# VectorE makes the first two one-hots of a stage before it waits for the chunk's dst sums and adds them

## The reference

```python
inv_dx = 1.0 / maximum(edge_attr_2[:, 0], 1e-6)
slope  = edge_attr_2[:, 1] * inv_dx
diff   = (x[dst] - x[src]) * inv_dx[:, None]
d1     = segment_sum(diff, dst) - segment_sum(diff, src)
S      = segment_sum(slope, dst)                  # the same for all features
x1     = layernorm(x + (x - clip(dt, 0.01, 2.0) * (x * d1 + g * S)))
mean   = segment_sum(edge_attr_16, dst) / max(count(dst), 1)
out    = layernorm(x1 + mean)
```

## Time and profile before

| | |
|---|---|
| median of three runs | 4510.34 us (4507.86 to 4515.13) |
| the profiled execution | 4508.76 us, of which 4506.9 us is the span from first to last instruction |
| granted TensorE clock, mean | 0.996 |
| TensorE matmul busy | 98% of the span |
| VectorE busy | 85% |
| GpSimd busy | 76% |
| ScalarE busy | 32% |
| first stage's head, last chunk's head | 56.1 us and 4418.8 us |

### The profile page before, as it was taken

The page is one execution under the profiler, slowest core; times in us unless marked ns, Lnnn a source line. Parts: engine busy times, 40 slices in busy tenths (PEclk is TensorE's granted clock), DMA queues, the critical chain, the costliest instruction groups (busy, mean ns, idle before and its releaser), DMA issues. The chain is left out here.

```text
span 4506.9 us, 73977 instructions
## 1 busy us (share of the span) xinstructions
PE 4409.8 (98%) x31379; PEld 1230.9 (27%) x12630; DVE 3846.0 (85%) x8605; ACT 1458.2 (32%) x1018; POOL 3430.4 (76%) x3133
## 2 busy tenths in 40 slices
PE   4999999999999999999999999999999999999997
PEld 1222222222222222222222222222222222222222
DVE  6888888888888888888888888888888888888887
ACT  4333333333333333333333333333333333333321
POOL 7777777777777777777777777777777777777770
PEclk9999999999999999999999999999999999999998
DMA  3111111111111111111111111111111111111110
GB/s 92 37 35 41 36 35 37 35 42 36 35 37 35 42 35 37 35 35 42 35 37 35 40 37 36 36 35 42 35 37 35 35 42 35 37 35 38 39 25 8
DMA packets 210291, 167.80 MB, mean 37 GB/s; under 512 B 124650, under 2 KB 193774, under 8 KB 210024
## 3 DMA queue, kind: packets, MB, share of 16 engines
q1 hardware_dynamic: 109798, 139.79, 10.1%
q0 software_dynamic: 100000, 25.80, 6.4%
q10 hardware_dynamic: 476, 2.01, 0.1%
HBM read 164.55 MB, written 2.81 MB: 37 GB/s over the span
## 5 line engine op out<-in xcount | busy, mean ns | idle before, releaser
L427 POOL DMA_INDIRECT x_src<-in_x_dram,src_i x3125 | 3425.4, 1096 | 961.5 <-issue 910.2
L653 PE MATMUL ps_src<-hi_hot,spread_lo 128*128 128x392 bf16 x18750 | 4125.1, 329 | 0.0
L1000 DVE TENSOR_SCALAR hi_hot<-col_h,hi_f,scale 128x1568 bf16<-128x1568 f16 x3125 | 2137.0, 703 | 23.9 <-PE ps_src L653 22.8
L648 PE MATMUL ps_src<-hi_hot,spread_lo 128*128 128x392 bf16 x6250 | 2048.9, 328 | 16.7 <-DVE hi_hot L1000 9.0
L648 PEld LDWEIGHTS ps_src<-hi_hot,spread_lo 128*128 128x128 f16 x6250 | 615.8, 99 | 1026.9 <-issue 648.0
L601 PEld LDWEIGHTS ps_w<-dst_hots,parts 128*102 128x102 bf16 x3125 | 392.5, 126 | 978.8 <-issue 939.3
L979 DVE TENSOR_TENSOR spread_lo<-spread_lo,halves 128x640 f16<-128x640 f16 x1250 | 601.7, 489 | 64.9 <-PE ps_src L653 64.8
L590 PEld LDWEIGHTS ps_x<-xwin,nodes_mem 112*128 112x128 bf16 x3125 | 301.4, 98 | 1197.6 <-issue 1187.8
L590 PE MATMUL ps_x<-xwin,nodes_mem 112*128 112x48 bf16 x3125 | 580.0, 188 | 13.7 <-ACT nodes_mem L530 13.7
L601 PE MATMUL ps_w<-dst_hots,parts 128*102 128x112 bf16 x3125 | 499.6, 213 | 4.0 <-DVE parts L908 4.0
L528 ACT ACTIVATE nodes_mem<-rel_all,row_neg 128x3200 bf16<-128x3200 f16 x125 | 370.2, 2962 | 393.1 <-PE ps_x L590 390.6
(11 more groups left out here) (119 smaller groups left out, 1110.8 us busy)
## 6 DMA issues: line engine op xcount, KB each, us to landing
rel_all<-rel_d SPq DMA_DIRECT2D x125, 800.0 KB
x_src<-in_x_dram,src_i POOLq DMA_INDIRECT x3125
a<-in_edge_attr_dram SPq DMA_DIRECT2D x125, 200.0 KB, 2.4
a<-in_edge_attr_dram SPq DMA_DIRECT2D x125, 25.0 KB
src_i<-in_src_dram SPq DMA_DIRECT2D x125, 12.5 KB, 1.9
dst_i<-in_dst_dram SPq DMA_DIRECT2D x125, 12.5 KB, 1.7
xwin<-xparts_d SPq DMA_DIRECT2D x125, 10.5 KB
dst_sum<-in_dst_dram SPq DMA_DIRECT2D x1, 1400.0 KB
```

Source lines behind the costliest of these rows:

```text
L427: nc.gpsimd.indirect_dma_start(x_src[:, b, j * F:(j + 1) * F], None, x[:, :], bass.IndirectOffsetOnAxis(ap=src_i[:, b, j:j + 1], axis=0)). ...
L648: return nc.tensor.matmul(out_bank, weights, moving, start=False, stop=stop)
L653: return nc.tensor.add_instruction(mybir.InstMatmult(name=nc.get_next_instruction_name(), engine=pe.engine, start_tensor_calc=False, stop_ ...
L1000: v.tensor_scalar(hi_hot[:, slot(j), :], col_h[:, :], hi_f[:, b, j:j + 1], scale[:, b, j:j + 1], ALU.is_equal, ALU.mult).then_inc(hi_hot_r ...
```

## The change

The call of `add_window` moves from ahead of the loop over j to behind one-hot 1. The register loads stay where they are. Everything that follows one-hot 1 in the stage keeps its order. The last chunk's own code (below the loop) is untouched.

```diff
+        WINDOW_AT = 1
...
                 dve.wait_ge(dve_step, base_step)
                 if tiles:
                     load_stage(c + 1)
-                    add_window(c, b, base_step)
-                    done["window_rel"] = count[0]
                 for j in range(J):
                     if tiles:
                         one_hot(c, b, j)
+                        if j == WINDOW_AT:
+                            add_window(c, b, base_step)
+                            done["window_rel"] = count[0]
                         late(c, j)
```

## The result

The changed kernel takes 4537.39 us (median of 4 executions, 4527.70 to 4540.58) against 4512.74 us for the kernel before (now the median of four, with 4517.24 as the fourth): 1.0055 times as long, 95% interval 1.0042 to 1.0069. That is slower, clear of noise, and outside the forecast range of 4504 to 4518. The profiled execution has a span of 4535.8 us, 28.9 more than before. By the heads of the stages, 1.8 us of it come up before stage 2, 27.1 us in the 122 stages from 2 to 123 (35.296 instead of 35.074 us each), nothing behind them.

The account below looks back on a forecast made before the run. TensorE's own work was taken to bound the kernel at 35.07 us a stage. Zero for TensorE and zero for the path at start and end gave 4510 us, own range 4507 to 4514, wider range 4504 to 4518.

Parts of the forecast that it names:

- What bounds the kernel: Whole run: TensorE's own work sets the stage at 35.07 us; VectorE has about 4.8 us idle in each.
- Do the one-hots fit?: Stage's head: moved one-hots start near 2032.5, end some 1.0 us before the sums; add stays at 2034.90, cost nothing.
- What VectorE gains: From one-hot 2 on VectorE may run 1.2 us earlier, given back at one-hot 20; its end of stage doesn't move.
- the wait before one-hot 20: Late in VectorE's stage: one-hot 20, come 1.2 us earlier, would wait about 1.1 us for tile 12.
- The gathers: GpSimd's gathers beside the moved one-hots: zero on balance, bounds -0.1 and +0.73 us of GpSimd's time a stage.
- Cost: 0: At the diff: 1.2 us earlier it waits 0.75 us for gathers; up to 2.7 us late is free for TensorE.
- Rival 2: GpSimd becomes the bound: stretched gathers delay the diff in all stages, 0.48 us a stage, 59 us, 4569 us; chance 0.12.
- Rival 1: TensorE's small waits, 4.8 us outside the first fill, go: 4505 to 4510 us, middle 4507; chance 0.10.
- Rival 3: Diff waits 1 to 3 us in all stages instead of 37; 3 us more, up to 8: 4513 to 4518; chance 0.10.
- Middle stages that are not 35.07 us apart: Sign of a wrong prediction; the gathers' mean against 1.097 and the diff's place against 2.7 us then test rival 2.

Follow-up runs that it names:

- scratch reduction: The kernel before with one extra 1.2 us tensor_reduce, its result unread, between the register loads and the wait for the dst sums: 4506.96 us, 0.9986 of the kernel before.
- run 5: The kernel before with the two spreads behind one-hots 2 and 3 moved behind one-hot 8, so the diff comes 0.8 us earlier: 4548.68 us, 1.0068 of the kernel before.

## Why the prediction was wrong

**What bounds the kernel.** TensorE, with VectorE idle 4.8 us a stage: right for the kernel before. The same part noted GpSimd's 35.0 us beside TensorE's 35.07, but as a remark to the gathers and not as a second bound.

**Do the one-hots fit?** The start near 2032.5, when tile 17 is done, was wrong. One-hot 0 starts on average 1.8 us behind the last slope (122.4 + 32.8 us in 86 waits, by the third and fourth row of VectorE's waits above), and in each of these stages within 0.14 us of the last register instruction, so it is these that it waits for and not TensorE, which the third row names. The register loads of `load_stage`, which stayed ahead of the one-hots, take that time on VectorE and were hidden under the wait of 3.8 us. So there is no 1.0 us between one-hots and add; the add follows at once and is itself up to some tenths late. Nobody waits for it, so this cost nothing here, as argued.

**What VectorE gains.** In the stage shown it did run ahead by 1.5 us up to the diff, and the wait before one-hot 20 doesn't appear, as the diff ate the lead first.

**The gathers: the step that failed.** The prediction wrote: "I take zero on balance, with bounds of -0.1 and +0.73 us of GpSimd's time a stage." It is +0.24: 25 gathers of 1.106 instead of 1.097, 27.66 us instead of 27.42. With 25 x 0.305 us between them that is 35.3 against TensorE's 35.07, and 122 stages of 0.22 are the 27 us. The bounds held it; the value was chosen by one gather beside one-hots (0.99), at the place that they leave, when the places that matter are those they come to: there the stretch is 0.36 us a chunk against 0.09. Nothing could take up 0.24 us, as the prediction had itself found: GpSimd's 35.04 stood beside TensorE's 35.07. The step before it failed too: a wait of 0.75 us for an earlier diff, "Cost: 0". The wait is 2.98, as the gathers fall behind until TensorE's own lateness stops them. Its 1.4 us from the end of the last gather to a waiting diff held: 3043.28 - 3041.81 = 1.47.

**Rival 2** named the mechanism, down to the chain of late diff, parts, tile 11, and had a chance of 0.12. Its price, 59 us, came from the three worst stages of the kernel before; the mean over good and bad stages is 0.22 a stage and not 0.48. As a cause it had the one-hots' new place in mind. The trace bears that out as to the place: the stretch was added at the head. But scratch one-hots at nearly the same place, with nothing brought forward, cost only 3 to 8 us, and an earlier diff with nothing in the gap cost about 31 (0.68%). So the two together, the moved one-hots and what runs earlier behind them, make the 25 us; how it divides between them is not shown. One reading, also not shown: when the diff waits, what stands ahead of it lies beside the very gathers that it waits for, and stretches these (1.14, 1.15, 1.21), while before the pattern had come to rest at a place with 0.94.

**Rival 1** (TensorE's small waits go) is wrong: they grew. **Rival 3** (the first regime lasts) is half of what one sees: the diff waits in all stages, but the regime itself became dearer, 7.93 us of TensorE's idle time in the first window where it was 1.24, so the price in the 85 stages from 37 on is 19 us and not 3 to 8.

Middle stages that are not 35.07 us apart were named as what would make the prediction wrong, with the gathers' mean against 1.097 and the diff's place as the test. The stages are 35.29 apart, the mean is 1.106, and in 26 of the 122 stages the diff starts more than 2.7 us behind its usual place: the test pointed to rival 2's chain.

## What to carry to other kernels

Before giving an engine's idle time to someone, list every engine whose own time for a stage lies within one per cent of the bound: here a second one, at 35.04 of 35.07, sat in a column that said 76% busy, because the 0.3 us between its instructions counts as idle. Such an engine need not have a fixed time for its stage: here it grew with the order of another's work. Work that comes earlier is no gain if it ends at a wait for that engine. An idle stretch can also hide instructions that the time line doesn't draw (1.8 us of register loads), so moving work into it needs that row too.

## What was not expected of the hardware

- The load of four registers from a table in SBUF, with the register work and the wait that belong to it, takes 1.3 to 2.0 us of VectorE's order (1.50 ahead of the scratch reduction, 2.04 ahead of one-hot 0).
- The gathers' length depends on where VectorE's instructions fall: the same 3125 gathers take a mean of 1.096 (before) to 1.111 us (run 5), with single ones from 0.94 to 2.27, and a reduction in their way leaves them alone (1.096).
- GpSimd's and TensorE's stage in the kernel before agree within 0.1% for 86 stages, though the trace shows no wait of the one for the other longer than 0.3 us. The chunk's last gather ends 5.16 to 5.84 us behind the head in each of stages 38 to 120. The gathers seem to fall into step with VectorE's order; no run took that apart.
